# An attention kernel on one core: ten groups of layer 1 as f32r halves, five of their low parts made by VectorE

## The reference

```python
# layer 0
theta, phi, g = theta_w @ x + theta_b, phi_w @ x + phi_b, g_w @ x + g_b    # 64 channels each
y = softmax(theta^T phi, axis=keys) @ g^T
x = W_w @ y^T + W_b + x
# layer 1
q, k, v = Wq @ x + bq, Wk @ x + bk, Wv @ x + bv                            # 128 channels each
x = x + (softmax(q^T k / sqrt(128), axis=keys) @ v^T)^T
```

## Time and profile before

| | |
|---|---|
| median of 3 runs | 3496.3 us (3496.25 to 3496.79) |
| profiled execution, its time | 3498.05 us |
| profiled execution, its span | 3496.2 us |
| TensorE matmul busy | 3410.6 us (98%) |
| VectorE busy | 2253.0 us (64%) |
| ScalarE busy | 1692.5 us (48%) |
| GpSimd busy | 2986.0 us (85%) |
| mean granted TensorE clock | 0.991 |

### The profile page before, as it was taken

How to read it: one execution, slowest core, us unless ns; L and a number is a source line. 1 busy time by engine, 2 the same in 40 slices (tenths; PEclk the granted TensorE clock), 3 DMA queues, 4 the chain that set the end, 5 groups by cost and what they waited for, 6 DMA issues and landing times.

```text
span 3496.2 us, 46705 instructions
## 1 busy us (share of the span) xinstructions
PE 3410.6 (98%) x13124; PEld 2071.4 (59%) x13124; DVE 2253.0 (64%) x3029; ACT 1692.5 (48%) x2241; POOL 2986.0 (85%) x1366
## 2 busy tenths in 40 slices
PE   7999999999999999999999999999999999999998
PEld 4445466666555446666654455666665444566665
DVE  4555567777655557676765555767676555677775
ACT  4454444444545444444445544444454545444444
POOL 4888789898988869899888886989898888698898
PEclk9999999999999999999999999999999999999999
DMA  1000000000000000000000000000000000000000
GB/s 42 13 18 19 28 7 22 15 22 16 19 16 18 16 26 13 19 17 19 13 19 19 18 16 23 16 16 21 16 19 13 19 18 16 19 13 10 18 11 11
DMA packets 34039, 61.73 MB, mean 18 GB/s; under 512 B 5281, under 2 KB 5921, under 8 KB 33569
## 3 DMA queue, kind: packets, MB, share of 16 engines
q1 hardware_dynamic: 33824, 59.23, 5.5%
HBM read 42.44 MB, written 16.78 MB: 17 GB/s over the span
## 4 chain that ended last, share of the span: by engine, by line
PE 91%; issue 3%; POOL 2%; DVE 2%; ACT 1%; SPq 0%; DVEq 0%; DMA 0%; ACTq 0%; POOLq 0%
PE acc_out L458 15%; PE acc_out L455 15%; PE rough L397 14%; PE scores L419 9%; PE scores L422 7%; PE scores L424 6%; PE scores L428 6%; PE scores L425 6%; PE acc_out L440 2%; PE acc_out L442 2%; PE acc_out L441 2%; POOL sums L279 2%; PE rough L379 2%; PE acc_out L467 1%; PE acc_out L385 1%
## 5 line engine op out<-in xcount | busy, mean ns | idle before, releaser
L279 POOL TENSOR_TENSOR sums<-sums,probs 128x1024 f32<-128x1024 f32 x886 | 2132.6, 2407 | 141.5 <-ACT probs L695 104.3
L770 DVE TENSOR_REDUCE piece_max<-rough 128x1 f32<-128x512 f32 x2024 | 1309.5, 684 | 631.2 <-PE rough L397 630.9
L787 DVE TENSOR_TENSOR probs<-scores,shift_rows 128x1024 f32<-128x1024 f32 x512 | 626.3, 1223 | 527.5 <-PE scores L428 495.9
L695 ACT ACTIVATE probs<-scores 128x1024 f32<-128x1024 f32 x512 | 524.5, 1024 | 684.6 <-PE scores L422 684.6
L688 ACT ACTIVATE probs<-probs 128x1024 f32<-128x1024 f32 x512 | 539.6, 1054 | 523.2 <-DVE probs L787 523.1
L889 POOL TENSOR_TENSOR p_lo<-probs,p_hi 128x1024 fp32r<-128x1024 f32 x192 | 462.9, 2411 | 178.6 <-ACT probs L688 178.2
L458 PE MATMUL acc_out<-probs,v_vals 128*128 128x512 f32 x1280 | 604.6, 595 | 0.0
L455 PE MATMUL acc_out<-probs,g_vals 128*64 128x512 f32 x2048 | 549.7, 617 | 0.0
L424 PE MATMUL scores<-qry_a,k_hi 128*128 128x512 f32 x1024 | 495.5, 484 | 0.0
L419 PE MATMUL scores<-qry_a,phi_a 128*128 128x512 f32 x1024 | 448.3, 438 | 0.0
L687 ACT ACTIVATE p_hi<-probs 128x1024 fp32r<-128x1024 f32 x192 | 203.5, 1060 | 440.2 <-DVE probs L787 414.2
(11 more groups left out here) (97 smaller groups left out, 3046.4 us busy)
## 6 DMA issues: line engine op xcount, KB each, us to landing
x_q<-x SPq DMA_DIRECT2D x32, 256.0 KB, 2.6
x_res<-x SPq DMA_DIRECT2D x32, 256.0 KB, 3.0
mid<-mid_new SPq DMA_DIRECT2D x32, 256.0 KB, 2.2
x_q<-mid SPq DMA_DIRECT2D x32, 256.0 KB, 2.8
x_res<-mid SPq DMA_DIRECT2D x32, 256.0 KB, 3.2
out<-result SPq DMA_DIRECT2D x32, 256.0 KB, 2.3
x_kv<-x SPq DMA_DIRECT2D x24, 256.0 KB, 2.6
probs<-x SPq DMA_DIRECT2D x2, 1024.0 KB, 6.1
```

Source lines behind the costliest of these rows:

```text
L279: eng.tensor_tensor(sums[:, parity], sums[:, parity], probs[:, s % P_BUFS], ALU.add).then_inc(s_plus, 1)
L770: nc.vector.reduce_max(piece_max[:, t, c:c + 1], src, AX.X).then_inc(s_reduced, 1)
L787: nc.vector.tensor_tensor(probs[:, s % P_BUFS].rearrange("p (h c) -> p h c", c=QB), scores[:, s % 2].rearrange("p (h c) -> p h c", c=QB), ...
```

## The change

Four things are changed.

- `HALVED` grows from the six groups 1, 3, 5, 9, 11, 13 to ten: GpSimd makes the low part for 1, 4, 7, 10, 13 (`POOL_LO`) and VectorE for 2, 5, 8, 11, 14 (`DVE_LO`), each with its own semaphore. Groups 2, 4, 7, 8, 10 and 14 leave the f32 product, and 3 and 9 come back to it.
- VectorE's `split_probs` for group `s - 1` stands in group `s` behind the shift and ahead of the pieces' reductions.
- `v_hi` and `v_lo` hold all keys now and not every second tile, since the halved groups are no longer only odd ones; the copy and the subtraction that fill them (`take_v`, `split_v`) are twice as wide.
- ScalarE writes `p_hi` for ten groups and not six (its code is the same).

```diff
-HALVED = (1, 3, 5, 9, 11, 13)
+POOL_LO, DVE_LO = (1, 4, 7, 10, 13), (2, 5, 8, 11, 14)
+HALVED = tuple(sorted(POOL_LO + DVE_LO))
...
-        v_hi = sb("v_hi", [P, BLOCKS, TPG * KT], F32R)
-        v_lo = sb("v_lo", [P, BLOCKS, TPG * KT], F32R)
+        v_hi = sb("v_hi", [P, N], F32R)
+        v_lo = sb("v_lo", [P, N], F32R)
...
-        s_p_lo = sem("s_p_lo")
+        s_p_lo = {POOL_LO: sem("s_p_lo_pool"), DVE_LO: sem("s_p_lo_dve")}
...
+        def lo_by(s):
+            return POOL_LO if s in POOL_LO else DVE_LO
+
         def halved(nth, s):
 
-            return nth * len(HALVED) + HALVED.index(s) + 1
+            by = lo_by(s)
+            return nth * len(by) + by.index(s) + 1
...
-                pe.wait_ge(s_p_lo, halved(nth, s))
+                pe.wait_ge(s_p_lo[lo_by(s)], halved(nth, s))
                 pe.wait_ge(l_v, (b + 1) * BLOCKS)
                 n = HALVED.index(s) % 2
                 for h in range(TPG):
-                    hi = v_hi[:, s // TPG, h * KT:(h + 1) * KT]
-                    lo = v_lo[:, s // TPG, h * KT:(h + 1) * KT]
+                    hi, lo = cols(v_hi, s * TPG + h, KT), cols(v_lo, s * TPG + h, KT)
...
-                copy(v_hi[:, bass.ds(c, 1)] if not isinstance(c, int) else v_hi[:, c:c + 1],
-                     src[:, TPG * KT:].unsqueeze(1))
+                copy(cols(v_hi, c), src)
                 copy(cols(v_vals, c), src).then_inc(h_v, 1)
...
+            def split_probs(g, s):
+
+                n = HALVED.index(s) % 2
+                dve.wait_ge(s_whole, whole_of(g, s))
+                nc.vector.tensor_tensor(p_lo[:, n], probs[:, s % P_BUFS], rd(p_hi[:, n]),
+                                        ALU.subtract).then_inc(s_p_lo[DVE_LO], 1)
+
...
                     if st.layer == 1:
                         shift_scores(st.g, st.nth, st.parity, s)
+                        if s - 1 in DVE_LO:
+                            split_probs(st.g, s - 1)
                     if st.nxt is not None:
                         for _ in range(min(at[s], 2)):
                             reduce_piece(st.pieces + m, pieces[m], two_banks(m))
...
-                at = bass.ds(c, 1) if not isinstance(c, int) else slice(c, c + 1)
-                lo_part(v_lo[:, at], cols(v_vals, 2 * c + 1, TPG * KT).unsqueeze(1), v_hi[:, at], l_v)
+                lo_part(cols(v_lo, c), cols(v_vals, c), cols(v_hi, c), l_v)
...
-                lo_part(p_lo[:, n], probs[:, s % P_BUFS], p_hi[:, n], s_p_lo)
+                lo_part(p_lo[:, n], probs[:, s % P_BUFS], p_hi[:, n], s_p_lo[POOL_LO])
...
-                    if st.layer == 1 and s in HALVED:
+                    if st.layer == 1 and s in POOL_LO:
                         split_probs(st.g, st.nth, s)
```

## The result

The changed kernel takes **3777.5 us** in the median of four runs (3767.4 to 3783.5), against 3496.3 before: a ratio of 1.080, 95% interval 1.079 to 1.082. It is slower, as forecast, but by 281 us and not by 135; 3777 lies above the whole range of 3545 to 3705.

A forecast was written before the change was run, and what follows sets the result against it. TensorE was taken to bound layer 1. Waits of 4W + 1.96 = 5.8 us a step, less 1.4 saved, gave 4.4 x 31 = 136, with edge corrections +135: 3633, median 3631 us, range 3545 to 3705.

The forecast's parts named there:

- TensorE's saving, less the third pieces of groups 7 and 10: Layer 1: four more halved groups net save 1.4 us a step; third pieces waiting for reductions take back 0.4.
- bare time of the subtractions: Layer 1: subtractions of 1.14 us ahead of the reductions, never held by GpSimd, delay TensorE 1.26 us a step.
- W: Wait of a VectorE instruction with two SBUF operands for GpSimd's running one: taken as 0.95 us, bounds 0 and 2.2.
- waits for GpSimd at TensorE's full clock: TensorE's delay from W in groups 3, 6, 9, 12, plus 0.3 us for the reciprocals' subtraction: +127 us.
- What bounds the kernel, and the sign: Layer 1: TensorE, busy 59.69 of 59.96 us a step, has nothing to spare; the change makes the kernel 3.9% slower.
- The saving: Layer 1: halved products cost 1.37 us against 1.72 for f32, saving 1.4 us a step, less 0.4 in groups 7, 10.
- The room of a group is VectorE's idle time before the next shift less 0.19: Time VectorE can add in a group before TensorE waits: 0.97 us in group 3, 0.92 in 6, 1.06 in 9.
- Its mean of 1.41 fits into the gap before shift 6: Group 6: the reciprocals' 128x4 subtraction waits 1.41 us in the mean, which fits; its longest doesn't, so 0.3 added.
- my cases: TensorE waits, 3555 to 3700 (0.71); no GpSimd wait, 3505 to 3555 (0.12); faster, 3453 (0.07); worse, 3786 (0.10).
- The worse case: W near 2.2 us each time, as GpSimd starts its next instruction when VectorE comes up: 3786 us, chance 0.10.
- GpSimd hidden: Layer 1: GpSimd, held five times but with one `p_lo` less, needs 56 us in a step of at least 58.5.
- my own list of signs: Layer 1: step 64.3 us, TensorE idle 5; subtractions mean 2.2, spread 1.22 to 3.5; 768 f32 passes; GpSimd additions to 3.3.

The follow-up runs named there:

- the kernel with one operand: Kernel after with each VectorE subtraction replaced by a maximum over the same 1024 columns, one SBUF operand, those low parts left zero: 3564.6 us, ratio 1.020.
- the filler: Kernel after plus 23 zero-weight matmuls in each interior layer 1 step, placed where TensorE would wait in groups 7, 10 and 12: 3732.8 us, ratio 1.068.
- the single kernels: Five kernels, each the kernel after with only one subtraction, other four low parts zero: group 3 3504.8, 6 3562.4, 9 3537.4, 12 3590.1, 15 3473.4 us.

## Why the prediction was wrong in size

The forecast and the runs, term by term, in us:

| term | forecast | runs |
|---|---|---|
| TensorE's saving, less the third pieces of groups 7 and 10 | -33 | -24 |
| bare time of the subtractions (1.14 us each, W = 0) | +39 | +92 |
| waits for GpSimd at TensorE's full clock | +127 | +126 to +168 |
| lower clock after long waits | 0 | +87 to +45 |
| sum | +133 | +281 |

The last two are the 213 us between the kernel with one operand and the kernel after, split by the filler (at least 45 for the clock) and by the granted clock (at most 87). So two terms are surely mis-sized, the bare time by 53 us and the clock by 45 at least; the waits for GpSimd may have been right. Before the small corrections at the edges my sum of the terms is 133.

- *What bounds the kernel, and the sign*: right. TensorE had nothing to spare in layer 1, and what it waits for is VectorE's reductions behind the subtractions.
- *The saving*: 0.74 us a step and not 1.4 - 0.4. That the values' products don't wait was right, and so was it that nothing follows in group 15 (1 us). ScalarE cost little, but not nothing: TensorE waits 0.53 us for its `phi_a` in group 11 of the step shown, 11 us over the whole execution.
- *"The room of a group is VectorE's idle time before the next shift less 0.19"*: this is the step that failed first. It gives the bare cost as 1.26 us a step; the kernel with one operand shows 62.5 - 59.2 = 3.3, of which 1.75 stand in groups 6 and 9. I took the idle times of groups 6 and 9 from one step of the kernel before. There the reciprocals' cast and subtraction took 0.19 and 0.17 us. In the changed kernel, with other groups halved, they take 0.75 and 2.29 even without any subtraction, and the residual 1602 ns in the mean against 982, so the idle time before shift 7 was gone.
- *"Its mean of 1.41 fits into the gap before shift 6"*: the mean was over 64 instructions, 32 of them in layer 0. It mixed waits of about 2.1 us in most of layer 0 with layer 1, where in the first three images 14 of 21 instructions took 0.16 or 0.17 us and the other seven 2.27 to 2.36, and it stood for no step at all. I should have read these instructions in the stretch of the change alone, and asked what they become when GpSimd's order changes.
- *W = 0.95*: right as a mean (0.89) and of little use. It is luck that it fits, for it came from other and smaller instructions, 64 of the 160 in layer 0. Measured alone, W is 0.20, 1.30, 1.06 and 1.91 us in groups 3, 6, 9 and 12, together 4.5 and not 3.8. The engines repeat the same meeting in every step, so the wait is no draw from a spread. Each of my cases gave one W to all four places. The worse case (3786) came near the time with a W of 2.2 everywhere, which is not what happened; only group 12 has it.
- *The clock*: missing altogether. I had seen it at 1.00 in the step and did not ask what long waits do to it. Waits so long were not in my sum either, since it spread 5.8 us over seven places; in the step shown three waits hold 7.4. The runs put the cost of the clock at 45 to 87 us.
- *GpSimd hidden*: held. It was busy for 55.9 us of the step, against my 56. But its order decides who waits.

By my own list of signs, the profile after showed subtractions with a mean of 2.1 us and a spread from 1.2 to 3.5, 768 f32 passes in layer 1 and GpSimd's longest addition in `sums` at 3.4 to 3.5 us, all about as written, but a step of 71.3 us and not 64.3. Still open is how the 126 to 168 us divide between the subtractions' own waits (4.5 x 31 = 139 by the single kernels) and those of the small instructions behind them, and why the five costs add up so well although they share the clock and the room.

## What to carry to other kernels

Where two engines meet on one resource in a loop, the meeting repeats: read the wait at each place of the loop in the stretch that the change touches, never as a mean over the program, and count the small instructions of the same kind, which a new order can turn from 0.2 us into 2.3. An idle gap that a change is to use is only there if what stands ahead of it keeps its length. A new instruction goes behind what the busiest engine waits for (here that took away 188 us of 281). And a long wait on TensorE is priced with the slower matmuls after it: here waits of 2.2 to 3.3 us were followed by them, though not in every step.

## What the runs showed of the hardware

- A conversion of 128x4 f32 with one SBUF operand waits for GpSimd as well: 0.17 us at the least, 1.31 in the step shown, ending at 1594.01 with GpSimd's instruction (1591.56 + 2.43 = 1593.99). The Trainium skill ("SBUF — State Buffer", Who interferes with whom) names casts among the instructions that can take the port pair shared with GpSimd; this row agrees. A maximum over 1024 columns never waited (1206 ns in the mean of 160).
- When VectorE is already waiting as GpSimd's instruction ends, either may come next. In group 6 of the kernel after, VectorE's subtraction waits from 1597.38 until GpSimd's additions end at 1598.76, goes next and ends at 1599.84, and GpSimd's `qry_b`, which takes 1.3 us alone, takes 2.25 (rows below). In group 12 of the kernel with that subtraction alone, VectorE is up 0.1 us before `phi_a` ends, GpSimd's addition goes next, and that costs 2.3 us. The same section says that the order of issue decides who is blocked. The first case agrees; in the second VectorE's start stands 0.08 us before the addition's, and it is held all the same. Why is not shown.
- Small shifts decide much. In the kernel before, the 128x4 subtraction starts at 2357.50, between two additions of GpSimd (the two take 4.91 us from 2355.02), and takes 0.17 us; in the kernel without subtractions it starts 0.1 us after such an addition and takes 2.29.
- In the step shown, TensorE waited 2.69 and 3.34 us (the earlier trace rows had no such wait), and the 3.60 and 4.66 us behind these waits have a granted clock of 0.53 and 0.63: a part of each ran at 1.2 GHz. After waits of 2.17 and 3.33 us it did so in some steps and not in others, in the kernels with one subtraction. With zero-weight matmuls in the waits it stayed at 2.4 GHz, and the kernel with 23 more matmuls a step was 45 us faster.

GpSimd in group 6 of the step of the kernel after:

```profile
1593.93 4.83 POOL L280 TENSOR_TENSOR sums<-sums,probs 128x1024 f32<-128x1024 f32 x2
1598.72 2.25 POOL L901 TENSOR_TENSOR qry_b<-q_whole,qry_a 128x512 fp32r<-128x512 f32 x1
```
